# Cross-attention and a mixture of experts on one core: softmax row sums from ScalarE's exponentials, their logarithm added to the maximum, and three chunks' maxima beside the projections

## The chip, the cores and the metric

The kernel runs on one core of a Trainium2 chip. The metric is the device time of one execution in microseconds. A core has TensorE (PE, matrix multiplications into PSUM), VectorE (DVE), ScalarE (ACT), GpSimd (POOL) and SyncE (SP, which here issues DMAs); each runs its own list of instructions in order, and they wait for each other by semaphores.

## The reference

The input x has 8 sequences of 512 tokens and 512 features, and so has the context. All is float32.

```
xn = layernorm(x)
Q = xn @ Wq.T + bq;  K = ctx @ Wk.T + bk;  V = ctx @ Wv.T + bv     # 16 heads of 32
attn = softmax(Q K^T / sqrt(32));  x = x + (attn V) @ Wo.T + bo
xn = layernorm(x)
scores = softmax(xn @ router.T + rb);  top 2 of 8 experts per token
x = x + sum over the two: score * (down( (up + 1) * gate * sigmoid(1.702 gate) ) + bias)
```

## The kernel before

The program has three stages one after the other: attention (`attention_stage`), the routing, and the experts. The change is in the first alone. It goes over the 8 sequences ("batches", b). Within one, the 512 features are four chunks c of 128 (four heads h of 32 each), and the 512 tokens four tiles t or k of 128.

**Precision.** Where float32 would be slow, a value is split in a high part of type float32r and a low part, and a product is made of three passes (`PASSES`, hi by hi, hi by lo, lo by hi). Each of q and k is split after its projection (`qk_hi` on ScalarE, line 430, and `qk_lo` on VectorE, line 595), and DMAs stack the parts in `qs[c]` and `ks[c]`, three by 32 rows of the contraction, so that one matmul of 96 rows is a head's product (`stack_hi` on SP's queue, `stack_lo` on GpSimd's, line 765). Two more rows of the contraction, 98 in all, hold the high and low part of minus the row maximum in `qs` and ones in `ks`: so the subtraction of the maximum is done by the matmul.

**Scores are made twice.** First by query: `row_max` (line 276) makes the scores of one head and 128 queries against 512 keys; VectorE takes their negated maximum (`reduce_max`, line 609) into `negmax`. Chunks 0 and 1 do it in pairs of query tiles, 128x1024 in a two-bank PSUM tile `st`; chunks 2 and 3 row by row, 128x512 in `work`. When a chunk's 16 maxima are there, `turn_max` transposes them, `m_hi_copy` and `m_lo_sub` split them, and `send_max` writes them into the two rows of `qs`. Then by key: `exp_scores` (line 291) makes the transposed scores of 128 keys, and ScalarE their exponential (line 448, with the scale 1/sqrt(32)) into `pt`. `weigh_values` multiplies these by v (`o_ps`, line 304) and by ones (`sum_ps`, line 309), the latter giving the row sums in the same layout. At a chunk's end `copy_sums` (line 457) copies both to SBUF, and in four pieces VectorE takes the reciprocal and multiplies (`divide`, lines 619 and 622), and the result is split into `oT` (`o_hi`, line 464; `o_lo`, line 627). `project_out` (line 326) multiplies by Wo: chunks 0 to 2 of all four token tiles first, then chunk 3.

**Order.** The order is written out by hand. `STEPS` lists twelve projections, k0 v0 q0 q1 k1 v1 q2 k2 v2 q3 k3 v3. Each is issued in four quarters, and after each quarter the function calls `next(fill)`: a generator that puts one item of other work there. The same generator skeleton stands on TensorE, ScalarE and VectorE, so that their orders agree. During the projections it puts in the previous batch's router work (transposes of `xln`, the logits, their sum), then chunk 0's maxima beside q2, k2, v2 and chunk 1's beside q3, k3, v3. During the weighing the items follow the 16 tiles (c, k), four places to a tile: the maxima of chunks 2 and 3, and the pieces of the division. In the last chunk's tiles VectorE also makes the next batch's statistics and LayerNorm (`norm_stats`, `ln1`, line 566), after which come the pieces that are left.

**Rings.** PSUM has 8 banks: `work` 2, `st` 2 tiles of two banks, `o_ps` and `sum_ps` one each. The uses of `work` and of `st` are listed in order (`use_work`, `use_st`), each takes the other buffer of two in turn, and a matmul waits until the use before the last has been read.

Of the kernel before, what the change touches and what calls it, by code (L numbers as in the profile page):

```python
# [14 lines left out]
P = 128  # L15
# [34 lines left out]
def attention_stage(nc, x, ctx_t, w_t, bq, bk, bv, bo, router_wt, router_b, out, xln_dram, logits, ident):  # L50
# [7 lines left out]
    with ExitStack() as ctx:  # L58
# [31 lines left out]
        o_sum = sb("o_sum", [P, 2, S])  # L90
        parts = sb("parts", [P, S])
        ones = sb("ones", [P, HD])
# [12 lines left out]
        o_ps = psum("o_ps", [P, S])  # L105
        sum_ps = psum("sum_ps", [P, S])

        STEPS = [(n, c) for c in range(C) for n in ("kvq" if c == 0 else "qkv")]
# [3 lines left out]

        bs = range(B)
        s_w, s_init, s_first_x, s_raw_w, s_split, s_split_lo = (sem(n) for n in (
            "w_in", "consts_made", "first_x_in", "raw_w_in", "w_hi_made", "w_lo_made"))
# [12 lines left out]
        MAXES = [(b, c, h, t) for b in bs for c in range(C) for h, t in (PAIRS if c < 2 else ROWS)]  # L128
# [13 lines left out]
        copied = Mark(sem("copied"), [(b, c, i) for b in bs for c in range(C) for i in (1, 0)])  # L142
        oT_hi_made = Mark(sem("oT_hi_made"), [(b, c, t) for b in bs for c in range(C) for t in range(T)])
# [12 lines left out]
        inverted = Mark(sem("inverted"), [(b, c, t) for b in bs for c in range(C) for t in range(T)])  # L156
        divided = Mark(sem("divided"), [(b, c, t) for b in bs for c in range(C) for t in range(T)])
        oT_lo_made = Mark(sem("oT_lo_made"), [(b, c, t) for b in bs for c in range(C) for t in range(T)])
# [15 lines left out]
        def use_st_for_router(b):  # L174
            for half in range(2):
                use_st((b, "xln", half), xlnT_made, (b, half))
            use_st((b, "logits"), parts_made, b)
            use_st((b, "sum"), logits_out, b)

        for b in bs:  # L180
            for n, c in STEPS:
                use_work((b, n, c), *((v_made, (b, c)) if n == "v" else (qk_lo_made, (b, n, c))))
                if (n, c) == ("q", 3):
                    use_work((b, "turn", 0), m_lo_made, (b, 0))
            for c in range(1, C):
                use_work((b, "turn", c), m_lo_made, (b, c))
                if c < C - 1:
                    for h, t in ROWS:
                        use_work((b, "max", c + 1, h, t), maxed, (b, c + 1, h, t))
# [4 lines left out]
            if b:  # L194
                use_st_for_router(b - 1)
            for c in range(2):
                for h, t in PAIRS:
                    use_st((b, "max", c, h, t), maxed, (b, c, h, t))
# [5 lines left out]
        use_st_for_router(B - 1)  # L204
# [3 lines left out]
        def on_pe(e):  # L208
# [15 lines left out]
            def turn_xln(b, half):  # L224
                i = take(st_ring, (b, "xln", half))
# [43 lines left out]
            def row_max(b, c, h, t):  # L269
                ring, n = (st_ring, 2) if c < 2 else (work_ring, 1)  # L270
# [8 lines left out]
            def turn_max(b, c):  # L279
                i = take(work_ring, (b, "turn", c))  # L280
                e.wait_ge(maxed.sem, maxed[(b, c, *(PAIRS if c < 2 else ROWS)[-1])])
                e.transpose(work[i][0:GROUP * T, 0:P], negmax[:, c, :], ident[:, :]).then_inc(max_turned.sem, 1)
# [13 lines left out]
            def weigh_values(b, c, k, fill):  # L296
                if k == 0:
                    e.wait_ge(v_made.sem, v_made[b, c])
                    if (b, c) != (0, 0):
                        e.wait_ge(copied.sem, copied[b if c else b - 1, c - 1 if c else C - 1, 0])  # L300
                e.wait_ge(exped.sem, exped[b, c, k, 1])
                for h in range(GROUP):
                    rows = slice(HD * h, HD * (h + 1))
                    e.matmul(o_ps[rows, :], v[:, k, c * P + HD * h:c * P + HD * (h + 1)], pt[k % 2][:, h, :],  # L304
                             start=(k == 0), stop=(k == T - 1))
                next(fill, None)
                for h in range(GROUP):
                    rows = slice(HD * h, HD * (h + 1))
                    ins = e.matmul(sum_ps[rows, :], ones[:, :], pt[k % 2][:, h, :], start=(k == 0), stop=(k == T - 1))  # L309
# [3 lines left out]
            def project_out(b):  # L313
# [4 lines left out]
                for chunks in (range(C - 1), range(C - 1, C)):  # L318
                    for t in range(T):
                        for c in chunks:  # L320
                            if c == C - 1:
                                e.wait_ge(oT_lo_made.sem, oT_lo_made[b, c, t])
                            elif t == 0:
                                e.wait_ge(oT_lo_made.sem, oT_lo_made[b, c, T - 1])
# [7 lines left out]
            def beside_first(b):  # L332
                for _ in range(7):
                    yield
                for half in range(2):
                    if b:
                        turn_xln(b - 1, half)
                    yield
                    yield
                yield  # L340
                if b:
                    route_logits(b - 1)
                for _ in range(4):
                    yield
                if b:
                    sum_logits(b - 1)
                yield

            def beside_second(b):
                yield  # L350
                for h, t in PAIRS:
                    row_max(b, 0, h, t)
                    yield

            def beside_third(b):
# [1279 lines left out]
```

## Time and profile before

| | us |
|---|---|
| median of 3 runs | 1897.19 (1895.81 to 1897.5) |
| profiled execution: its time | 1896.04 |
| profiled execution: its span | 1894.3 |
| TensorE, VectorE, ScalarE, GpSimd busy | 1735.4, 1366.4, 667.7, 469.7 |
| exponentials (line 448), 256 | 249.4 |
| row maxima of 128x512 (line 609), 256 | 175.0 |
| row maxima of 128x1024 (line 609), 128 | 151.6 |
| reciprocals (line 619), 128 | 120.9 |
| matmuls into sum_ps (line 309) | 135.0 |

Matmuls are pipelined: the duration of one in the trace is longer than the distance from its start to the next one's start, and the distances are what adds up. The same holds for instructions of ScalarE and VectorE that follow each other without a wait.

### The profile page before, as it was taken

What the parts mean: (1) busy time and instruction counts of PE and PEld (TensorE: products, weight loads), DVE (VectorE), ACT (ScalarE), POOL (GpSimd) and SP (SyncE); (2) the same over time, 40 slices, a digit from 0 to 9 for tenths busy, and PEclk for the clock granted to TensorE, in tenths of its full rate; (3) what the DMA queues carried; (4) which work ended last, traced back from release to release, by engine and by line L of the source; (5) the groups of instructions that cost most, each with busy time, mean ns of one, the idle gap of its engine ahead of it and who ended that gap; (6) DMA issues with size and microseconds to landing.
All of it is one profiled execution on the core that took longest, in us unless ns stands there. A gap on an engine that the chain in (4) does not pass through costs nothing. (4 is left out here: it accounts for less than half of the span.)

```text
span 1894.3 us, 31367 instructions
## 1 busy us (share of the span) xinstructions
PE 1735.4 (92%) x10597; PEld 1253.6 (66%) x10597; DVE 1366.4 (72%) x2488; ACT 667.7 (35%) x1107; POOL 469.7 (25%) x628
## 2 busy tenths in 40 slices
PE   5989989989989999899899827999999999999996
PEld 4537547447356365375474427998989889889895
DVE  3775775775766757757757587778787888888874
ACT  2252342441532622523524404233434343434221
POOL 3212113013022032121122002343333333334332
PEclk9999999999999999999999958999999999999998
DMA  6404306206117025044052042253636535636322
GB/s 220 127 2 135 111 1 169 77 25 171 52 44 202 2 76 170 2 119 127 1 141 62 36 145 80 69 218 101 227 92 224 201 124 191 216 123 230 92 79 78
DMA packets 103797, 216.06 MB, mean 114 GB/s; under 512 B 25936, under 2 KB 26960, under 8 KB 103632
## 3 DMA queue, kind: packets, MB, share of 16 engines
q1 hardware_dynamic: 75696, 135.27, 22.4%
q0 software_dynamic: 27936, 78.73, 13.2%
q8 instruction: 86, 1.41, 0.3%
q14 instruction: 79, 0.65, 0.1%
HBM read 204.19 MB, written 37.36 MB: 128 GB/s over the span
## 5 line engine op out<-in xcount | busy, mean ns | idle before, releaser
L1265 PE MATMUL gu_ps<-xgT_hi,wg_hi 128*128 128x256 f32 x1248 | 354.9, 284 | 0.0
L1265 PE MATMUL gu_ps<-xgT_hi,wg_lo 128*128 128x256 f32 x1248 | 351.7, 282 | 0.0
L1265 PE MATMUL gu_ps<-xgT_lo,wg_hi 128*128 128x256 f32 x1248 | 351.5, 282 | 0.0
L448 ACT ACTIVATE pt<-st 128x1024 f32<-128x1024 f32 x256 | 249.4, 1018 | 152.2 <-PE st L291 152.2
L1265 PEld LDWEIGHTS gu_ps<-xgT_hi,wg_hi 128*128 128x128 f32 x1248 | 235.5, 189 | 0.0
L1265 PEld LDWEIGHTS gu_ps<-xgT_lo,wg_hi 128*128 128x128 f32 x1248 | 235.5, 189 | 0.0
L1265 PEld LDWEIGHTS gu_ps<-xgT_hi,wg_lo 128*128 128x128 f32 x1248 | 235.3, 189 | 0.0
L609 DVE TENSOR_REDUCE negmax<-work 128x1 f32<-128x512 f32 x256 | 175.0, 689 | 62.4 <-PE work L276 61.3
L1325 ACT ACTIVATE sig<-gate 128x256 f32<-128x256 f32 x156 | 65.0, 417 | 303.1 <-DVE gate L1377 303.1
L291 PE MATMUL st<-qs,ks 98*128 98x512 f32 x512 | 165.1, 416 | 5.8 <-ACT pt L448 5.1
L609 DVE TENSOR_REDUCE negmax<-st 128x2 f32<-128x1024 f32 x128 | 151.6, 1218 | 25.6 <-PE st L276 23.9
L1503 POOL DMA_INDIRECT out<-acc,idx x78 | 77.3, 991 | 346.8 <-DVE acc L1413 346.8
L1278 PE MATMUL d_ps<-wd_hi,hid_hi 128*128 128x512 f32 x312 | 127.3, 408 | 22.9 <-DVE acc L1410 22.9
L755 POOL TENSOR_TENSOR var_eps<-mv,eps_col 128x4 f32<-128x4 f32 x16 | 3.2, 197 | 571.5 <-DVE mv L563 571.4
L260 PE MATMUL work<-ctxT,wk 128*128 128x512 f32 x256 | 128.4, 610 | 13.0 <-DVE q_lo L595 8.7
L304 PE MATMUL o_ps<-pt,v 128*32 128x512 f32 x1024 | 136.2, 604 | 2.3 <-issue 2.3
L619 DVE RECIPROCAL o_sum<-o_sum 128x128 f32<-128x128 f32 x128 | 120.9, 944 | 23.9 <-ACT o_sum L457 23.9
L291 PEld LDWEIGHTS st<-qs,ks 98*128 98x128 f32 x512 | 88.7, 189 | 70.7 <-ACT pt L448 38.3
L309 PE MATMUL sum_ps<-pt,ones 128*32 128x512 f32 x1024 | 135.0, 598 | 0.0
L257 PEld LDWEIGHTS work<-wv,ctxT 128*128 128x128 f32 x1024 | 123.1, 192 | 11.2 <-issue 7.7
L1278 PE MATMUL d_ps<-wd_lo,hid_hi 128*128 128x512 f32 x312 | 125.3, 401 | 0.0
L1278 PE MATMUL d_ps<-wd_hi,hid_lo 128*128 128x512 f32 x312 | 125.1, 401 | 0.0
(195 smaller groups left out, 3170.5 us busy)
## 6 DMA issues: line engine op xcount, KB each, us to landing
raw_g<-w_gate_up SPq DMA_DIRECT2D x39, 2048.0 KB
raw_d<-w_down SPq DMA_DIRECT2D x39, 1024.0 KB
ks<-k_hi SPq DMA_DIRECT2D x256, 64.0 KB, 2.1
qs<-q_hi SPq DMA_DIRECT2D x256, 64.0 KB, 2.5
bd<-b_down SPq DMA_DIRECT2D x39, 256.0 KB
x_in<-x SPq DMA_DIRECT2D x8, 1024.0 KB, 5.3
ctxT<-ctx_t SPq DMA_DIRECT2D x8, 1024.0 KB, 5.7
ks<-k_lo POOLq DMA_DIRECT2D x128, 64.0 KB, 2.4
```

The costliest lines, as they stand in the source:

```text
L257: ins = e.matmul(work[i][:, k * P:(k + 1) * P], ctxT[:, kk, k * P:(k + 1) * P], wv[:, kk, c * P:(c + 1) * P], start=(kk == 0), stop=(kk == ...
L260: ins = e.matmul(work[i][:, :], wk[:, k, c * P:(c + 1) * P], ctxT[:, k, :], start=(k == 0), stop=(k == C - 1))
L291: ins = e.matmul(st[i][:, j, :], ks[c][0:3 * HD + 2, h, k * P:(k + 1) * P], qs[c][0:3 * HD + 2, h, :], start=True, stop=True)
L304: e.matmul(o_ps[rows, :], v[:, k, c * P + HD * h:c * P + HD * (h + 1)], pt[k % 2][:, h, :], start=(k == 0), stop=(k == T - 1))
L309: ins = e.matmul(sum_ps[rows, :], ones[:, :], pt[k % 2][:, h, :], start=(k == 0), stop=(k == T - 1))
L448: e.activation(pt[k % 2][:, 2 * p:2 * p + 2, :], st[st_ring.bank[b, "exp", c, k, p]][:, :, :], ACT.Exp, scale=scale).then_inc(exped.sem, 1)
L609: e.tensor_reduce(negmax[:, c, h * T + t:h * T + t + n], src, AX.X, ALU.max, negate=True).then_inc(maxed.sem, 1)
L619: e.reciprocal(o_sum[:, 1, cols], o_sum[:, 1, cols]).then_inc(inverted.sem, 1)
L1265: ins = e.matmul(gu_ps[n % GU_BANKS][:, part, :], wg[s][pw][:, k, cols], xgT[s][px][:, k, :], start=(k == 0 and m == 0), stop=(k == KD - 1 ...
L1278: ins = e.matmul(d_ps[j][:, :], hid[s][px][:, k, j * P:(j + 1) * P], wd[s][pw][:, k, :], start=(k == 0 and m == 0), stop=(k == KF - 1 and ...
L1325: e.activation(sig[f % 2][:, :], gate[f % 2][:, :], ACT.Sigmoid, scale=ALPHA).then_inc(sig_made.sem, 1)
L1503: e.indirect_dma_start(out=out_rows, out_offset=slot_rows(i, j), in_=acc[i % 2][:, j, :], in_offset=None).then_inc(scattered.sem, 16)
```

## The change

- `sum_ps`, its matmuls, `ones`, `o_sum`, the copies, the reciprocals and the multiplications are removed. The 256 matmul groups of `weigh_values` into `o_ps` stay, and `o_ps` has two buffers now, by the parity of the chunk. One copy (`o_hi`) and one subtraction (`o_lo`) of 128x512 make `oT` straight from `o_ps`.
- The row sums are made on the scores by query: after VectorE's maximum, ScalarE takes the exponential of the same PSUM tile in place, with the negated maximum as its bias, and its accumulator output gives the sum of a row (`row_sums`: 64 per batch, 128x512 each). The PSUM buffer is free only after that.
- Per chunk, ScalarE takes the logarithm of the 16 columns of sums (`ln_of_sums`) and VectorE subtracts it from the negated maximum (`add_ln`); this `shift` is what is transposed and sent. So the exponentials by key are normalised already.
- The scale 1/sqrt(32) goes into Wq and bq at the start.
- Three chunks' row maxima (24 pairs) stand beside the projections instead of two; chunk 3's alone stand row by row in the weighing. The order of steps is k0 q0 q1 k1 k2 q2 q3 k3 v0 v1 v2 v3. A quarter counts from 0 to 47; chunk c's pairs stand at 12(c + 1) + 0, 1, 3, 4, 6, 7, 9, 10, the turns of chunks 0 and 1 at 26 and 38, the router's work at 8, 10, 14 and 17.
- GpSimd sends the maxima of chunks 0 and 1 after all its stacking; SP stores the previous batch's rows after k1.

```diff
-        STEPS = [(n, c) for c in range(C) for n in ("kvq" if c == 0 else "qkv")]
+        STEPS = [(n, c) for c in range(C) for n in ("kq" if c % 2 == 0 else "qk")] + [("v", c) for c in range(C)]
+        PAIR_AT = {12 * (c + 1) + n // 2 * 3 + n % 2: (c, *PAIRS[n]) for c in range(C - 1) for n in range(len(PAIRS))}
+        TURN_AT = {12 * (c + 2) + 2: c for c in range(C - 2)}
+        ROUTER_AT = {8: ("xln", 0), 10: ("xln", 1), 14: "logits", 17: "sum"}
...
             def weigh_values(b, c, k, fill):
                 if k == 0:
-                    e.wait_ge(v_made.sem, v_made[b, c])
-                    if (b, c) != (0, 0):
-                        e.wait_ge(copied.sem, copied[b if c else b - 1, c - 1 if c else C - 1, 0])
+                    e.wait_ge(v_made.sem, v_made[b, C - 1])
+                    if c >= 2:
+                        e.wait_ge(oT_lo_made.sem, oT_lo_made[b, c - 2])
+                    elif b:
+                        e.wait_ge(oT_lo_made.sem, oT_lo_made[b - 1, c + 2])
                 e.wait_ge(exped.sem, exped[b, c, k, 1])
-                for h in range(GROUP):
-                    rows = slice(HD * h, HD * (h + 1))
-                    e.matmul(o_ps[rows, :], v[:, k, c * P + HD * h:c * P + HD * (h + 1)], pt[k % 2][:, h, :],
-                             start=(k == 0), stop=(k == T - 1))
                 next(fill, None)
                 for h in range(GROUP):
                     rows = slice(HD * h, HD * (h + 1))
-                    ins = e.matmul(sum_ps[rows, :], ones[:, :], pt[k % 2][:, h, :], start=(k == 0), stop=(k == T - 1))
+                    ins = e.matmul(o_ps[c % 2][rows, :], v[:, k, c * P + HD * h:c * P + HD * (h + 1)], pt[k % 2][:, h, :],
+                                   start=(k == 0), stop=(k == T - 1))
...
+            def row_sums(b, c, h, t):
+                ring, n = (st_ring, 2) if c < C - 1 else (work_ring, 1)
+                i = ring.bank[b, "max", c, h, t]
+                e.wait_ge(maxed.sem, maxed[b, c, h, t])
+                for j in range(n):
+                    at = h * T + t + j
+                    scores = st[i][:, j, :] if n == 2 else work[i][:, :]
+                    e.activation(scores, scores, ACT.Exp, bias=negmax[:, c, at:at + 1],
+                                 accum_out=sums[:, c, at:at + 1]).then_inc(summed.sem, 1)
+
+            def ln_of_sums(b, c):
+                e.wait_ge(summed.sem, summed[(b, c, *ROWS[-1])])
+                e.activation(ln_sums[:, c, :], sums[:, c, :], ACT.Ln).then_inc(ln_made.sem, 1)
...
+            def beside_projections(b):        # ScalarE
+                for quarter in range(C * len(STEPS)):
+                    if b and quarter in ROUTER_AT:
+                        what = ROUTER_AT[quarter]
+                        if what == "logits":
+                            parts_copy(b - 1)
+                        elif what != "sum":
+                            xln_copy(b - 1, what[1])
+                    if quarter - 1 in PAIR_AT:
+                        row_sums(b, *PAIR_AT[quarter - 1])
+                    if quarter + 1 in TURN_AT:
+                        ln_of_sums(b, TURN_AT[quarter + 1])
+                    if quarter in TURN_AT:
+                        m_hi_copy(b, TURN_AT[quarter])
                     yield
...
+            def beside_weighing(b):           # ScalarE
+                yield
+                ln_of_sums(b, C - 2)
+                yield
+                m_hi_copy(b, C - 2)
+                yield
+                for h, t in ROWS:
                     yield
+                    row_sums(b, C - 1, h, t)
                     yield
+                ln_of_sums(b, C - 1)
                 yield
+                m_hi_copy(b, C - 1)
                 yield
...
+            def add_ln(b, c):
+                e.wait_ge(ln_made.sem, ln_made[b, c])
+                e.tensor_tensor(shift[:, c, :], negmax[:, c, :], ln_sums[:, c, :], ALU.subtract).then_inc(shift_made.sem, 1)
...
+            def o_lo(b, c):
+                e.wait_ge(oT_hi_made.sem, oT_hi_made[b, c])
+                e.tensor_tensor(oT[1][:, c, :], o_ps[c % 2][:, :], oT[0][:, c, :].bitcast(F32), ALU.subtract).then_inc(oT_lo_made.sem, 1)
...
-                    if (n, c) == ("q", 3):
-                        send_max(e, b, 0)
-                send_max(e, b, 1)
+                for c in range(C - 2):
+                    send_max(e, b, c)
```

## Rows read from the trace of the kernel before

**Rows 1.** The page's totals: busy us (share of the span), count.
```profile
PE 1735.4 (92%) x10597; PEld 1253.6 (66%) x10597; DVE 1366.4 (72%) x2488; ACT 667.7 (35%) x1107; POOL 469.7 (25%) x628
```
**Rows 2.** Busy time by stretch: stretch, length, engines, TensorE clock, DMA.
```profile
400.01:419.92 19.91, 15.79 (x68) 12.41 (x65) 15.44 (x24) 2.99 (x7) 3.78 (x1) 0.83 0.00 1
419.92:472.65 52.73, 51.50 (x276) 37.91 (x274) 32.65 (x42) 9.69 (x14) 17.97 (x36) 1.00 0.61 173
472.65:533.21 60.56, 59.14 (x358) 22.70 (x356) 42.63 (x80) 36.89 (x53) 2.94 (x5) 1.00 0.13 43
405.00:411.00 6.00, 5.30 (x13) 4.19 (x14) 4.32 (x9) 1.70 (x4) 0.00 (x0) 0.52 0.01 3
```
**Rows 3.** Timeline of TensorE, output projection: start, us, line, count, idle before.
```profile
401.27 0.40 PE L326 MATMUL work<-wo_hi,xT_hi 128*128 128x512 f32 x1
405.70 0.80 PE L326 MATMUL work<-wo_hi,oT_hi 128*128 128x512 f32 x1 [4.03 <-DVE xT_hi L627]
...
418.12 1.97 PE L221 MATMUL st<-ident,x_in 128*128 128x128 f32 x16
419.92 3.60 PE L260 MATMUL work<-ctxT,wk 128*128 128x512 f32 x8
...
1065.78 0.51 PE L326 MATMUL work<-wo_hi,oT_hi 128*128 128x512 f32 x1
...
1076.80 0.40 PE L326 MATMUL st<-wo_hi,xT_hi 128*128 128x512 f32 x1
```
**Rows 4.** Timeline of VectorE around the same output projection.
```profile
395.14 2.47 DVE L558 BATCH_NORM_STATS2 stats<-x_in 128x6 f32<-128x512 f32 x4
...
399.31 6.14 DVE L566 TENSOR_SCALAR x_in<-x_in,mv,rstd 128x512 f32<-128x512 f32 x4 [1.43 <-POOL rstd L757]
405.37 0.28 DVE L627 TENSOR_TENSOR xT_hi<-o_sum,oT_hi 128x128 fp32r<-128x128 f32 x1
...
421.34 2.33 DVE L582 TENSOR_TENSOR xT_lo<-st,xT_hi 128x1024 fp32r<-128x1024 f32 x2
```
**Rows 5.** Timeline of TensorE, a tile of the weighing without row maxima.
```profile
515.30 1.20 PE L291 MATMUL st<-qs,ks 98*128 98x512 f32 x4
516.43 1.06 PE L304 MATMUL o_ps<-pt,v 128*32 128x512 f32 x8
517.32 1.04 PE L309 MATMUL sum_ps<-pt,ones 128*32 128x512 f32 x8
518.29 0.50 PE L291 MATMUL st<-qs,ks 98*128 98x512 f32 x1
```
**Rows 6.** Groups of ScalarE by shape, 387 to 517: busy us, mean ns, idle.
```profile
L448 ACT ACTIVATE pt<-st 128x1024 f32<-128x1024 f32 x31 | 30.2, 1018 | 19.0 <-PE st L291 19.0
...
L430 ACT ACTIVATE q_hi<-work,bq_col 128x512 fp32r<-128x512 f32 x4 | 2.7, 687 | 11.0 <-PE work L263 11.0
...
L457 ACT ACTIVATE o_sum<-sum_ps 128x512 f32<-128x512 f32 x4 | 2.4, 598 | 10.4 <-DVE xT_hi L627 7.9 <-PE sum_ps L309 2.5
...
L438 ACT ACTIVATE m_hi<-work 16x128 fp32r<-16x128 f32 x4 | 1.0, 254 | 4.9 <-PE work L282 4.9
```
**Rows 7.** Timeline of ScalarE, two exponentials in sequence.
```profile
387.05 1.92 ACT L448 ACTIVATE pt<-st 128x1024 f32<-128x1024 f32 x2
```
**Rows 8.** Groups of ScalarE over the whole span: both table loads.
```profile
L513 ACT ACT_TABLE_LOAD x1 | 1.3, 1283 | 2.0 <-PEq L1578 2.0
L1325 ACT ACT_TABLE_LOAD x1 | 1.3, 1283 | 0.0
```
**Rows 9.** Timeline of TensorE, projections: quarters of k, pairs of row maxima.
```profile
447.56 1.02 PE L260 MATMUL work<-ctxT,wk 128*128 128x512 f32 x2
448.02 1.02 PE L276 MATMUL st<-ks,qs 96*128 96x512 f32 x2
448.89 1.02 PE L260 MATMUL work<-ctxT,wk 128*128 128x512 f32 x2
...
459.68 0.62 PE L276 MATMUL st<-ks,qs 96*128 96x512 f32 x2
460.14 0.40 PE L263 MATMUL work<-xT_hi,wq_hi 128*128 128x512 f32 x1
```
**Rows 10.** Timeline of VectorE, the maximum of the pair of 459.68.
```profile
460.34 1.22 DVE L609 TENSOR_REDUCE negmax<-st 128x2 f32<-128x1024 f32 x1 [1.28 <-PE st L276]
```
**Rows 11.** Timeline of GpSimd, issuing the stack of a low part of q.
```profile
433.44 1.96 POOL L765 DMA_DIRECT2D qs<-q_lo  x4 [4.95 <-DVE q_lo L595]
```
**Rows 12.** DMA issues, 387 to 517: count, KB each, median us to landing.
```profile
qs<-q_lo POOLq DMA_DIRECT2D x16, 64.0 KB, 2.3
```

More of the change, by code:

```diff
@@ L172, in use_st, with use_st_for_router @@
             st_uses.append((key, len(st_uses) % 2, mark, event))
[L174 to L178, printed above, removed]
+        ROUTER_AT = {8: ("xln", 0), 10: ("xln", 1), 14: "logits", 17: "sum"}
+        def use_st_for_router(b, what):
+            over = {"logits": (parts_made, b), "sum": (logits_out, b)}
+            use_st((b, what), *over.get(what, (xlnT_made, (b, what[1]))))
         for b in bs:
-            for n, c in STEPS:
+            for i, (n, c) in enumerate(STEPS):
                 use_work((b, n, c), *((v_made, (b, c)) if n == "v" else (qk_lo_made, (b, n, c))))
-                if (n, c) == ("q", 3):
[L184 to L189, printed above, removed]
+                for quarter in range(C * i, C * (i + 1)):
+                    if quarter in TURN_AT:
+                        use_work((b, "turn", TURN_AT[quarter]), m_lo_made, (b, TURN_AT[quarter]))
+            use_work((b, "turn", C - 2), m_lo_made, (b, C - 2))
+            for h, t in ROWS:
+                use_work((b, "max", C - 1, h, t), summed, (b, C - 1, h, t))
+            use_work((b, "turn", C - 1), m_lo_made, (b, C - 1))
             for t in range(2):
@@ L203, in attention_stage @@
                 use_st((b, "out", t), x2_made, (b, t))
-        use_st_for_router(B - 1)
+        for what in ROUTER_AT.values():
+            use_st_for_router(B - 1, what)
         work_ring, st_ring = Ring(work_uses), Ring(st_uses)
@@ L224, in turn_xln @@
             def turn_xln(b, half):
-                i = take(st_ring, (b, "xln", half))
+                i = take(st_ring, (b, ("xln", half)))
                 for j in range(2):
@@ L416, in xln_copy @@
                 e.wait_ge(xln_turned.sem, xln_turned[b, half])
-                e.activation(pt[0][:, 2 * half:2 * half + 2, :], st[st_ring.bank[b, "xln", half]][:, :, :],
+                e.activation(pt[0][:, 2 * half:2 * half + 2, :], st[st_ring.bank[b, ("xln", half)]][:, :, :],
                              ACT.Identity).then_inc(xlnT_made.sem, 1)
@@ L473, in beside_first, with beside_projections @@
-            def beside_first(b):
-                for _ in range(7):
+                e.activation(oT[0][:, c, :], o_ps[c % 2][:, :], ACT.Identity).then_inc(oT_hi_made.sem, 1)
+            def beside_projections(b):
+                for quarter in range(C * len(STEPS)):
+                    if b and quarter in ROUTER_AT:
+                        what = ROUTER_AT[quarter]
+                        if what == "logits":
+                            parts_copy(b - 1)
[5 more added lines that the diff above has]
+                        ln_of_sums(b, TURN_AT[quarter + 1])
+                    if quarter in TURN_AT:
+                        m_hi_copy(b, TURN_AT[quarter])
+                    yield
@@ L511, in on_act @@
             e.wait_ge(s_raw_w, 32)
-            for w, raw in ((wq, pt[0]), (wo, pt[1])):
-                e.activation(w[0][:, :, :], raw[:, :, :], ACT.Identity).then_inc(s_split, 1)
+            for w, raw, factor in ((wq, pt[0], scale), (wo, pt[1], 1.0)):
+                e.activation(w[0][:, :, :], raw[:, :, :], ACT.Identity, scale=factor).then_inc(s_split, 1)
             for b in bs:
@@ L604, in reduce_max @@
             def reduce_max(b, c, h, t):
-                n, ring, banks = (2, st_ring, st) if c < 2 else (1, work_ring, work)
+                n, ring, banks = (2, st_ring, st) if c < C - 1 else (1, work_ring, work)
                 i = ring.bank[b, "max", c, h, t]
```

277 lines of the change are left out of this document (80 added, 197 removed).

## The prediction, made before the change was run

> **What bounds the kernel now.** I read the page's totals first, then the busy time by stage, then the order of work on each engine in one batch. TensorE is the busiest engine, at 92% of the span, with VectorE at 72% and ScalarE at 35% [rows 1]. One batch of the attention stage takes 133.2 us, from 400.01 to 533.21, in three stages [rows 2]: the output projection with the transposes of the next x, 19.9 us; the projections of k, v and q, 52.7; the weighing, 60.6. In the last two TensorE is busy 98% of the time, so there its work sets the time. The first is different: the output projection stands still for 4.03 us, waiting for the low part of oT [rows 3], because VectorE first runs the statistics and the LayerNorm of the next x, from 395.14 to 405.37 [rows 4]. Around this stall the granted clock is 0.52 on average [rows 2], the lower of the two levels (1.2 and 2.4 GHz) for a part of it. In the last batch, which has no next x, the same 48 matmuls run from 1065.78 to 1076.80, 11.3 us with the last one's slot [rows 3]. ScalarE is busy 9.7 of 52.7 us in the projections and 36.9 of 60.6 in the weighing [rows 2].
>
> **What is removed, stage by stage.** I count from the time of the profiled execution, 1896.04 us (its span is 1894.3; the median of the runs shown is 1897.19, so 1.2 us above it).
>
> Output projection: the four reciprocals, multiplications and splits of the last chunk become one copy and one subtraction. VectorE reaches the next x's statistics right after the low part of chunk 2, about four tiles before the end of the weighing. Statistics, the wait for rstd (1.43) and the LayerNorm take 10.2 us [rows 4]; four tiles take some 9 (4 x 2.1, and the last weighing). The low part of chunk 3 is then ready about 4 us after the last tile, and 36 matmuls of chunks 0 to 2 at 0.235 us (11.3 over 48) cover 8.5 us. So the stall and the low clock behind it go. 11.3 + 1.8 for the transposes (from 418.12 to the end of the stage at 419.92) [rows 2, 3] + 0.4 of gaps + 0.3 waiting for the low half of the next x = 13.8 us instead of 19.9: 6.1 gained, in 7 batches, since the last had no stall. That is 42.7 us.
>
> Weighing: today a tile without row maxima takes 2.99 us (515.30 to 518.29), of which the sum matmuls are 0.97 (517.32 to 518.29) [rows 5]. Without them, and with 16 row maxima instead of 32, TensorE needs 2.0 us in such a tile, and some 2.5 where two row maxima of 0.23 stand in it (a pair takes 0.46, from 459.68 to 460.14) [rows 9]. ScalarE now sets the pace. An exponential of 128x1024 takes 1.02 us by itself and 0.92 in sequence (two end after 1.92; 1.92 - 1.00) [rows 6, 7]. A row's sum is a new operation: an exponential of 128x512 with a bias column and an accumulator output. No row shows the output. Call its slot R. The nearest row is q_hi, 128x512 with a bias column, 0.687 us, which is 0.59 with the same overlap of 0.1 [rows 6]. That is the lower bound: the accumulator costs nothing. The upper one adds the whole of the shortest ScalarE row, m_hi with 128 columns (0.254), and no overlap: 0.94. I take the accumulator as m_hi without its columns: 0.254 - 128 x 0.00082 = 0.15 (0.00082 us a column: 1018 less 598 ns over 512 columns is 0.82 ns) [rows 6], so R = 0.74, which of the two ends lies nearer to the q_hi row. Then: start 2.0 (the last pair of chunk 2 goes out 1.4 us before the projections end, and its bank is held 3.5); first tile 1.84; eight tiles with rows, 8 x (1.84 + 2 x 0.74) = 26.6; seven without at 2.1 (TensorE's 2.0 and a handoff), 14.7; three copies of o_ps on ScalarE, 0.5 each and one of them partly beside TensorE, 1.2; two logarithms and two m_hi at 0.16 after overlap, 0.7; the last weighing, 0.9 and a handoff, 1.0. Sum 48.0 instead of 60.6: 12.6 gained per batch. With R = 0.59 it is 45.6, with 0.94 it is 51.2. VectorE, busy 42.6 of 60.6 us there today [rows 2], loses the divisions and half of the row maxima and isn't late.
>
> **What is added: the projections.** Here are now 24 pairs of rows instead of 16, and each pair's bank is held for more. Before: matmuls to the start of the reduction 0.66 us (459.68 to 460.34; the matmuls end at 460.30, so a handoff costs 0.04), reduction 1.22 [rows 9, 10], then free. Now two exponentials follow: hold = 0.66 + 1.22 + two handoffs, 0.08, + 2R + the last one's overlap, 0.1 = 3.54 us. Two banks make two pairs per 3.54 us. TensorE's own time for two pairs and the three quarters between them: a quarter of k with its pair takes 1.33 (447.56 to 448.89) of which the pair is 0.46 [rows 9], so with k 3 x 0.87 + 0.94 = 3.55, with v about the same, with q (three matmuls of 0.235) 3.04. So in k and v the ring just keeps up, and every disturbance of it is paid. I wrote the order of the three engines out, quarter by quarter. TensorE's bare work is 52.7 + 8 pairs x 0.5 - 1.1 of today's wait for q_lo = about 55. The stalls that I find on top:
> - quarter 12: the pairs of chunk 0 start one step after q0. Its low part is ready 1.6 us after the projection, GpSimd's four issues take 1.96 and the landing 2.3 [rows 11, 12], against q1, the xln transposes and a k quarter (5.3): 0.9;
> - the router's two uses of the same ring (the xln transposes before them have it to themselves), at quarters 14 and 17, wait for sums ahead of them, and ScalarE's copy of the logits stands before the sums of pair 13: 0.8 + 1.3 + 1.3;
> - the q quarters of q2, with the splits of q and k in between: 1.2;
> - quarter 26: the transposition of the maxima now waits for reduction, sums, logarithm and addition of the last pair of chunk 0, queued behind pair 24: 1.4. Behind it k3 waits for q3's split, which stands behind these sums on ScalarE and behind the addition on VectorE: 1.6;
> - chunk 1's last two pairs 0.7, its turn at quarter 38 1.0, v2's bank 0.4, chunk 2's last pair 0.4.
>
> That is 11 at R = 0.69, where I wrote it out, and 12 at R = 0.74 (12 rounds of the ring by 0.1). Projections: 67.0 instead of 52.7, 14.3 lost per batch. With R = 0.59, 63.9; with R = 0.94, 12 x 0.4 more, 71.9.
>
> Costed at nothing: the order k, q, q, k with v last (the low half of x is made at 423.67, and k0 covers from 419.92 until 423.52, so q0 waits the 0.3 counted above [rows 3, 4]; v is needed only at the first weighing); the later send of the maxima of chunk 0 on GpSimd (some 3 us for two sends, done about 5 us before ScalarE's next m_hi; if it were late, ScalarE's queue, with the sums behind it, would wait); the store of xln one step earlier on SP's queue, behind which the stacking of k2 and q2 lies, needed more than 10 us later; the scale put into wq at the start, the same two instructions as before; k's and q's stacks for chunk 1, three steps old.
>
> **Sum.** 8 x (12.6 - 14.3) = -13.6, and 42.7: a gain of 29 us, 1867 us. At R = 0.59: 8 x (15.0 - 11.2) + 42.7 = 73, 1823. At R = 0.94: 8 x (9.4 - 19.2) + 42.7 = -36, 1932.
>
> **Rivals.**
> 1. The hold is lighter (R near 0.59, or ScalarE's and VectorE's turns fall better than I wrote them): 1823. For it: handoffs of 0.04 leave nothing between the engines to lose. If the ring never bound at all, the projections would take 56 us, and the time would be 1896 - 42.7 - 8 x (12.6 - 3.3) = 1779. Against that: 3.54 us of hold against 3.04 in q.
> 2. The sums are dear, R above 0.83: there the gain is spent (0.1 of R is worth 8 x (2.4 + 1.6) = 32 us). Place: the bank held in the projections and ScalarE's queue in the weighing. Up to 1932. For it: the unknown accumulator. Against: 0.83 is already 0.24 above the activation's slot.
> 3. The logarithm and the exponential don't share a table. Then each of the 32 logarithms brings a load and one back, 64 x 1.28 us [rows 8] = 82 us on the queue that holds the ring: 1867 + 82 = 1949. It decides from 0.9 us per logarithm. Against: in the attention stage's trace Identity and Exp run after a single load [rows 8].
>
> The Trainium skill bears on this last one ("ScalarE: Activation LUTs", Table sets: the hidden batching unit): one set, natural_log_exp_and_others, holds both, so exponential after logarithm needs one load; and "ScalarE activation tables: per-element evaluation and per-set limits" (Table sets in the compiler and the runtime) says that the back end takes the set with the longest run. By that rule rival 3 doesn't happen. The first page gives 2.66 us for a switch with its drain; by that price the rival would stand at 1867 + 170. No row before has a logarithm, so that the rule holds here is not shown.
>
> **How the numbers follow.** Forecast, 1840 to 1893: 0.55. Rival 1: 0.15 for 1800 to 1840, 0.04 for less. No measurable change, within 0.2% (3.8 us, about what a measurement of this kernel can tell from none): 0.04. Rival 2: 0.13. Rival 3: 0.09. Faster 0.74, same 0.04, slower 0.22. The range goes from 1815 to 1925: it leaves out rival 3, the last of rival 2, and the lightest of rival 1. The forecast's own range is 1840 to 1893. With the 1.2 us between execution and median I give 1868.
>
> **What would show it.** Right: no wait of 4 us in the output projection, its clock 1.0, and 14 us for that stage; 48 us for the weighing with ScalarE the busiest engine; about 67 us for the projections, with TensorE waiting for ScalarE's sums before the pairs, at the two turns and before k3; sums of about 0.7 us plus a short accumulator entry. Wrong: a table load beside the logarithms; R off by more than 0.1; the stall in the output projection still there, because VectorE comes to the next x later than I think; projections under 60 us.

## The result, and the profile after

The changed kernel takes 2046.92 us (median of 4 runs, 2044.52 to 2048.85), the one before 1897.35 on the same chip: a ratio of 1.0788 [1.0769, 1.0807], 7.9% slower. I had forecast 1868. The profiled execution has a span of 2047.1 us, and a mean granted clock of 0.911 where the kernel before had 0.962.

The page's totals (busy us, share, instructions) after; [rows 1] are those of before:

```profile
PE 1725.3 (84%) x9573; PEld 1249.2 (61%) x9573; DVE 1205.9 (59%) x2105; ACT 1064.6 (52%) x2067; POOL 471.4 (23%) x627
```

TensorE's share fell from 92 to 84%, ScalarE's rose from 35 to 52%. No engine is at its limit over the whole; something waits. The same batch as in [rows 2], by its three stages (stretch, length, busy time of TensorE, its weight loads, VectorE, ScalarE, GpSimd, then granted clock, DMA share, GB/s):

```profile
459.89:473.20 13.31, 13.23 (x68) 10.76 (x65) 8.20 (x12) 1.27 (x2) 2.02 (x1) 1.00 0.01 2
473.20:552.66 79.46, 63.60 (x292) 43.66 (x290) 42.91 (x53) 47.76 (x113) 18.98 (x38) 0.89 0.42 120
552.66:610.09 57.43, 46.77 (x210) 16.90 (x210) 19.53 (x34) 49.99 (x79) 3.76 (x3) 0.88 0.12 38
```

| stage, us | before | forecast | after |
|---|---|---|---|
| output projection and transposes | 19.9 | 13.8 | 13.3 |
| projections | 52.7 | 67.0 | 79.5 |
| weighing | 60.6 | 48.0 | 57.4 |
| one batch | 133.2 | 128.8 | 150.2 |

The first stage is as forecast. The other two are longer by 12.5 and 9.4 us, and 8 x 21.4 is 171 of the 179 us that were missing. Both have a clock well below 1.0, which in [rows 2] only the first stage had.

These groups of ScalarE are new; nothing in [rows 6, 8] is like them (line, operation, count, busy us, mean ns, idle time before and its releaser):

```profile
L438 ACT ACTIVATE st<-st,negmax 128x512 f32<-128x512 f32 x384 | 252.7, 658 | 157.7 <-DVE negmax L571 156.8
...
L443 ACT ACT_TABLE_LOAD x32 | 41.1, 1283 | 0.6
...
L438 ACT ACTIVATION_READ_ACCUMULATOR st<-st,negmax 128x1 f32 x384 | 76.2, 198 | 0.0
...
L438 ACT ACT_TABLE_LOAD x16 | 20.5, 1283 | 0.3
L427 ACT ACT_TABLE_LOAD x16 | 20.5, 1283 | 13.8 <-PE o_ps L313 13.7
```

There are 64 table loads in attention: one ahead of each of the 32 logarithms (line 443), and one ahead of the exponential that follows each, half of those being row sums (438) and half exponentials of the weighing (427). This is rival 3. ScalarE in order of time shows both new things, the sum's slot and the round trip of a logarithm (start, us, instruction, idle time before it):

```profile
400.94 0.66 ACT L438 ACTIVATE st<-st,negmax 128x512 f32<-128x512 f32 x1 [0.44 <-DVE negmax L571]
401.53 0.19 ACT L438 ACTIVATION_READ_ACCUMULATOR st<-st,negmax 128x1 f32 x1
401.62 0.65 ACT L438 ACTIVATE st<-st,negmax 128x512 f32<-128x512 f32 x1
...
405.90 1.28 ACT L443 ACT_TABLE_LOAD   x1
407.19 0.22 ACT L443 ACTIVATE ln_sums<-sums 128x16 f32<-128x16 f32 x1
407.43 1.28 ACT L427 ACT_TABLE_LOAD   x1
```

From one sum to the next, 400.94 to 401.62, are 0.68 us: R, with the accumulator's entry partly under the next exponential. The logarithm of 0.22 us holds ScalarE for 2.8.

What TensorE waited for in this batch (total us, times, longest):

```profile
PE work L288 <- DVE shift L576: 12.2, 4, 5.3
PE st L282 <- DMA qs<-q_hi: 4.3, 1, 4.3
PE st L282 <- ACT st L438: 2.6, 5, 1.0
PE work L266 <- DVE q_lo L557: 2.5, 1, 2.5
PE st L297 <- ACT st L438: 1.2, 2, 0.9
...
PE st L251 <- ACT st L438: 1.1, 1, 1.1
```

The rings that I had costed at length cost 3.7 us in the projections: 2.6 before pairs (line 282) and 1.1 before the router's logits (line 251). In the weighing they cost another 2.3: 1.2 before the first exponentials (line 297) and 1.1 before a row of chunk 3. The largest wait is for `shift`, the maxima with the logarithm added, at the four transpositions: 2.46, 2.38, 2.03 and 5.30 us in their order. The next is for chunk 0's `q_hi` to land. TensorE in order of time shows these stalls and, at the end, tiles of the weighing:

```profile
489.77 1.19 PE L282 MATMUL st<-ks,qs 96*128 96x512 f32 x2 [4.26 <-DMA qs<-q_hi]
...
520.94 2.07 PE L266 MATMUL work<-ctxT,wk 128*128 128x512 f32 x2 [2.54 <-DVE q_lo L557]
...
565.17 1.31 PE L297 MATMUL st<-qs,ks 98*128 98x512 f32 x4
...
568.33 1.31 PE L297 MATMUL st<-qs,ks 98*128 98x512 f32 x4
...
591.82 0.37 PE L288 MATMUL work<-ident,shift 128*16 128x128 f32 x1 [5.30 <-DVE shift L576]
...
597.46 1.20 PE L297 MATMUL st<-qs,ks 98*128 98x512 f32 x4
...
599.59 1.37 PE L297 MATMUL st<-qs,ks 98*128 98x512 f32 x4
```

A tile with two row sums takes 3.16 us (565.17 to 568.33), one without 2.13 (597.46 to 599.59). In the row at 520.94 the two matmuls take 2.07 us, where two of the same shape took 1.02 before [rows 9]. The stretches right behind three of the stalls, in the columns of the stages:

```profile
489.70:495.70 6.00, 5.93 (x16) 2.65 (x16) 2.45 (x2) 1.45 (x4) 0.00 (x0) 0.59 0.32 82
520.90:526.70 5.80, 5.76 (x11) 2.96 (x12) 2.53 (x3) 2.90 (x8) 1.97 (x4) 0.62 0.51 136
591.80:597.40 5.60, 5.58 (x21) 1.65 (x21) 0.28 (x1) 3.48 (x4) 0.00 (x0) 0.54 0.01 3
```

TensorE is busy all through them at a granted clock of 0.54 to 0.62, that is for most of each at 1.2 GHz instead of 2.4. So these stalls seem to be paid twice, by their length and by the low clock behind them; e2 and e11 below test this.

What holds q_hi up is to be seen in SyncE's queue of DMA issues, after:

```profile
477.56 4.97 SPq L742 DMA_DIRECT2D ks<-k_hi  x8
482.62 10.18 SPq L742 DMA_DIRECT2D qs<-q_hi  x16
```

Eight issues take 4.97 us, 0.62 each. The queue does k0's eight until 482.5, then q0's, the first half of the sixteen in the second row, to about 487.6, and these land at 489.7. The same price stood in the same queue of the kernel before, a row that I had not drawn on:

```profile
424.27 4.96 SPq L815 DMA_DIRECT2D ks<-k_hi  x8
```

### The profile page after: what moved, and what is told of

Its sections match the earlier page's. It is cut to its first block and busy times, and to the rows that moved or that the text cites. A ratio compares the mean times of both kernels' runs of the same rounds, so it can differ in the third digit from the quotient of the medians.

```text
span 2047.1 us, 29620 instructions
## 1 busy us (share of the span) xinstructions
PE 1725.3 (84%) x9573; PEld 1249.2 (61%) x9573; DVE 1205.9 (59%) x2105; ACT 1064.6 (52%) x2067; POOL 471.4 (23%) x627
## 5 line engine op out<-in xcount | busy, mean ns | idle before, releaser
L438 ACT ACTIVATE st<-st,negmax 128x512 f32<-128x512 f32 x384 | 252.7, 658 | 157.7 <-DVE negmax L571 156.8
L571 DVE TENSOR_REDUCE negmax<-st 128x2 f32<-128x1024 f32 x192 | 234.0, 1222 | 136.4 <-PE st L282 135.1
L282 PE MATMUL st<-ks,qs 96*128 96x512 f32 x384 | 177.9, 548 | 57.6 <-DMA qs<-q_hi 38.0
L297 PE MATMUL st<-qs,ks 98*128 98x512 f32 x512 | 181.1, 461 | 10.8 <-ACT st L438 9.3
L266 PE MATMUL work<-ctxT,wk 128*128 128x512 f32 x256 | 159.3, 733 | 21.7 <-DVE q_lo L557 17.1
L313 PE MATMUL o_ps<-pt,v 128*32 128x512 f32 x1024 | 156.4, 687 | 4.6 <-ACT pt L427 4.6
L282 PEld LDWEIGHTS st<-ks,qs 96*128 96x128 f32 x384 | 73.4, 217 | 124.3 <-issue 78.7
L263 PEld LDWEIGHTS work<-wv,ctxT 128*128 128x128 f32 x1024 | 134.5, 200 | 12.3 <-DVE v L563 5.3
L571 DVE TENSOR_REDUCE negmax<-work 128x1 f32<-128x512 f32 x128 | 87.4, 688 | 90.3 <-PE work L282 90.3
L263 PE MATMUL work<-wv,ctxT 128*128 128x128 f32 x1024 | 137.6, 285 | 0.3 <-DVE v L563 0.3
```

Of the source, the lines that this page charges most:

```text
L263: ins = e.matmul(work[i][:, k * P:(k + 1) * P], ctxT[:, kk, k * P:(k + 1) * P], wv[:, kk, c * P:(c + 1) * P], start=(kk == 0), stop=(kk == ...
L266: ins = e.matmul(work[i][:, :], wk[:, k, c * P:(c + 1) * P], ctxT[:, k, :], start=(k == 0), stop=(k == C - 1))
L282: ins = e.matmul(to, qs[c][0:3 * HD, h, (t + j) * P:(t + j + 1) * P], ks[c][0:3 * HD, h, :], start=True, stop=True)
L297: ins = e.matmul(st[i][:, j, :], ks[c][0:3 * HD + 2, h, k * P:(k + 1) * P], qs[c][0:3 * HD + 2, h, :], start=True, stop=True)
L313: ins = e.matmul(o_ps[c % 2][rows, :], v[:, k, c * P + HD * h:c * P + HD * (h + 1)], pt[k % 2][:, h, :], start=(k == 0), stop=(k == T - 1))
L438: e.activation(scores, scores, ACT.Exp, bias=negmax[:, c, at:at + 1], accum_out=sums[:, c, at:at + 1]).then_inc(summed.sem, 1)
```

## The experiments

My theory after the traces: three things cost the time, the loads (64 x 1.28 = 82 us by themselves), the new waits (`shift`, and q_hi on SP's queue) and the clock that falls behind them. The rival: the sums themselves, in rings and ScalarE's queue, cost it, and the waits are only where it shows.

**One table.** ScalarE's table is loaded by hand once at the start, with the set that holds both functions:

```
+            e.add_instruction(mybir.InstLoadActFuncSet(..., engine=Activation, act_func_set_id=6))
             e.wait_ge(s_raw_w, 32)
```

> The changed kernel with one table that holds both Exp and Ln loaded at the start, so that the 64 loads beside the logarithms go. Theory A (the loads are the largest part of the loss: 64 x 1.28 us stand on the way, and after each the clock of TensorE is low for some us): 1935 to 1965 us, no load in the attention stage, the waits at the turns 1.3 us shorter each. Rival B (the ring is what holds, the loads lie beside waits that stay): above 2010 us.

1960.33 us, 1.0334 [1.0317, 1.0352] of before: 87 us less than the change. No load stands beside the logarithms any more:

```profile
375.00 1.95 ACT L427 ACTIVATE pt<-st 128x1024 f32<-128x1024 f32 x2
376.85 0.21 ACT L443 ACTIVATE ln_sums<-sums 128x16 f32<-128x16 f32 x1
376.95 1.02 ACT L427 ACTIVATE pt<-st 128x1024 f32<-128x1024 f32 x1
```

The round trip went from 2.8 us to 0.1. The loads, with what they drag behind them, explain half of the missing 179. The rest stands in this kernel's projections, weighing, and waits:

```profile
441.10:513.43 72.33, 60.47 (x292) 41.63 (x290) 42.80 (x53) 42.08 (x109) 18.91 (x38) 0.95 0.46 132
513.43:567.71 54.28, 46.48 (x210) 16.40 (x210) 19.62 (x34) 44.58 (x75) 3.75 (x3) 0.91 0.11 40
...
549.30:555.10 5.80, 5.80 (x22) 1.57 (x21) 0.28 (x1) 2.21 (x3) 0.00 (x0) 0.50 0.01 3
```

```profile
PE work L288 <- DVE shift L577: 6.5, 4, 3.9
...
PE st L282 <- DMA qs<-q_hi: 4.2, 1, 4.2
...
PE work L266 <- DVE q_lo L558: 1.1, 1, 1.1
```

The wait for shift halved, its longest still 3.9 us, and the stretch behind that one runs at 0.50. The wait for q_hi is untouched.

**The clock by itself.** Throwaway matmuls fill the stalls at the turns and before the first pair, and the waits stay (the one before k3 is left unfilled). This is done first on the changed kernel (e2), then, with fewer, on the one-table kernel (e11):

```
                 i = take(work_ring, (b, "turn", c))
+                for _ in range(9 if c < 2 else (8 if c == 2 else 22)):   # second: 4, 4, 2, 16
+                    e.matmul(work[i][:, :], wq[0][:, 0, 0:P], wq[0][:, 1, :], start=True, stop=True)
                 e.wait_ge(shift_made.sem, shift_made[b, c])
...
+                if (c, h, t) == (0, 0, 0):
+                    for _ in range(18):
+                        e.matmul(st[i][:, 0, :], wq[0][:, 0, 0:P], wq[0][:, 1, :], start=True, stop=True)
                 e.wait_ge(stacked[c].sem, stacked[c][b])
```

> The changed kernel with throwaway matmuls of 128x512 (0.235 us each) on TensorE before its five long waits of a batch: 18 before the first pair of chunk 0, 9 before the turns of chunks 0 and 1, 8 and 22 before those of chunks 2 and 3. The waits stay as long as they are, TensorE only works through them. Theory A (after a wait of 2 us or more the clock falls for some 6 us, which costs up to 2 us of TensorE's own time each, in the projections where it is near the limit): 1990 to 2015 us and a granted clock near 1.0 in the attention stage. Rival C (the clock's fall is hidden, since ScalarE and the ring set the pace): 2040 to 2055 us with the clock high all the same.

2000.52 us, 1.0554 [1.0532, 1.0575]: 46 less than the change, the mean clock up from 0.911 to 0.966.

> e1_one_table with throwaway matmuls before its long waits (18 before chunk 0's first pair, 4, 4, 2 and 16 before the four turns). Theory A on the clock: the low clock after the two waits of about 4 us costs some 1 to 2 us each, so 15 to 35 us less than 1960; granted clock of the attention stage near 1.0. Rival C (hidden): within 8 us of 1960.

1916.82 us, 1.0107 [1.009, 1.0124]: 43.5 less than one table alone, clock 0.97 instead of 0.94, and more than the 15 to 35 that I expected. Work that yields nothing made the kernel 2.2% faster. The weighing went from 54.3 us to:

```profile
495.19:545.22 50.03, 46.64 (x229) 18.68 (x229) 19.54 (x34) 44.50 (x75) 3.76 (x3) 1.00 0.13 44
```

Filler can't shorten a wait by itself; what changed is the clock, here 1.00 instead of 0.91.

**The sums themselves.** One table, and chunks 0 to 2 leave out the exponentials of their row sums (one-column exponentials signal in their place):

```
+                if n == 2:
+                    for j in range(n):
+                        at = h * T + t + j
+                        e.activation(sums[:, c, at:at + 1], negmax[:, c, at:at + 1], ACT.Exp, scale=0.0)...
+                    return
```

> As e1_one_table, and the row sums of chunks 0 to 2 are left out (one column of ones is written instead of the two exponentials), so that a pair's PSUM buffer is free about 0.3 us after its maximum. It leaves out part of the softmax. Theory A: the hold of the ring costs 8 to 12 us of a batch's projections; 65 to 95 us less than e1_one_table. Rival D (the ring hardly binds, the turns and the DMAs do): less than 30 us below e1_one_table.

1904.24 us, 1.0038 [1.0024, 1.0052]: 56 below one table, less than expected. The projections go to 66.7 us a batch. So 384 of the 512 sums cost 56 us, some of which the forecast had counted, and even without them the projections are 14 us longer than before. As the loads cost 87 us and were no part of this, the rival is not the main cause of the miss; it is no small one either.

**Cover for q_hi by another order of steps.** v0 is put between q0 and the pairs:

```
-        STEPS = [(n, c) for c in range(C) for n in ("kq" if c % 2 == 0 else "qk")] + [("v", c) for c in range(C)]
+        STEPS = [(n, int(c)) for n, c in "k0 q0 v0 q1 k1 k2 q2 v1 q3 k3 v2 v3".split()]
```

> The changed kernel with the steps k0 q0 v0 q1 k1 k2 q2 v1 q3 k3 v2 v3 (GpSimd sends chunk 0's maxima after q3's stack), so that 3.6 us more lie between q0 and chunk 0's first pair. Theory E (the 4.3 us wait before that pair is SP's issuing: 16 descriptors of k0 and q0 at 0.62 us one after the other): the wait is below 1 us, and the time 2000 to 2020 us. Rival (the transfers themselves are late, for lack of bandwidth): the wait stays above 3 us and the time within 1% of 2047.

2046.89 us, 1.0790 [1.0764, 1.0816]: nothing, and a miss. v0 only took the place of q1 between q0 and the first pair, so it added hardly any cover. In the batch looked at the wait is 3.0 us instead of 4.3, put down to the issue itself:

```profile
PE st L282 <- issue: 3.0, 1, 3.0
```

The run says nothing for or against the queue; the edit was badly made.

**The issues on two queues.** One table, and GpSimd issues the second copy of chunk 0's high parts, which SP did before:

```
-                for part in places:
+                for part in places[:1] if c == 0 else places:          # SP
...
+                if c == 0:                                              # GpSimd, ahead of the low part
+                    e.wait_ge(qk_hi_made.sem, qk_hi_made[b, n, c])
+                    for r in range(GROUP):
+                        e.dma_start(dst[HD * part:HD * (part + 1), r, :]..., hi[n][c % 2][...]...).then_inc(stacked_too.sem, 16)
```

> As e1_one_table, and for chunk 0 alone the second copy of the high parts is issued by GpSimd, so that SP issues 4 descriptors of k0 and of q0 instead of 8, and GpSimd 8 of 0.5 us. Theory E (the wait before chunk 0's first pair is issuing time in a queue): q0's last part now lands by GpSimd's queue, some 1.4 us sooner; the wait falls from 4.4 to about 3 us, and the time by 8 to 20 us, to 1940 to 1952. Rival F (the landing is late for another reason, the transfers' bandwidth or q0's split): the wait and the time stay within 4 us of e1_one_table, 1960.

1937.48 us, 1.0213 [1.0196, 1.023]: 23 less than one table. The wait went from 4.2 to 1.9 us, and is now for GpSimd's low part:

```profile
PE st L285 <- DMA qs<-q_lo: 1.9, 1, 1.9
```

So the wait was the queue's issuing, 0.62 us a descriptor. 2.3 us x 8 are 18 of the 23; that the rest is the clock is argued and was not tried here.

**The turns later.** One table; each transposition of the maxima stands later, by one quarter in the projections and by four and five places (a tile or a little more) in the weighing, its result goes into the `o_ps` bank that is idle then, and the logarithm goes ahead of the next chunk's sums:

```
-        TURN_AT = {12 * (c + 2) + 2: c for c in range(C - 2)}
+        TURN_AT = {12 * (c + 2) + 3: c for c in range(C - 2)}
...
-                e.transpose(work[i][0:GROUP * T, 0:P], shift...
+                e.transpose(o_ps[TURN_IN[c]][0:GROUP * T, 0:P], shift...
...
+                    if quarter + 3 in TURN_AT:                  # ScalarE, ahead of row_sums
+                        ln_of_sums(b, TURN_AT[quarter + 3])
...
+                    if at == 7:                                 # TensorE, places in the weighing (before: 3 and 37)
+                        turn_max(b, C - 2)
+                    if at == 42:
+                        turn_max(b, C - 1)
```

> As e1_one_table, and the transposition of a chunk's shifts comes later on TensorE, where logarithm and addition are done (quarters 27 and 39; places 7 and 42 of the weighing instead of 3 and 37), the logarithm stands ahead of the next chunk's sums, and the result goes into an idle o_ps bank instead of the ring of work. Theory G (the turns' waits, 6.2 us of a batch, k3's wait of 1.1 and the low clock behind them are the second part of the loss): 8 to 11 us of a batch, 1870 to 1900 us, no wait for shift over 0.3 us. Rival H (ScalarE sets the pace and the waits only move to other places): above 1935 us.

1926.88 us, 1.0163 [1.0146, 1.018]: 33.5 less than one table, not the 60 to 90 expected. The wait for shift is gone, but others grew in its place:

```profile
PE st L278 <- DMA qs<-q_hi: 4.1, 1, 4.1
PE st L278 <- ACT st L435: 4.1, 6, 1.5
...
PE st L296 <- ACT pt L424: 1.9, 3, 1.4
```

The ring's wait for ScalarE went from 2.6 in the changed kernel to 4.1: TensorE, no longer held at the turns, now meets the sums. That is one part of the shortfall. The other is the clock, as two weighings of this one execution show:

```profile
224.78:273.74 48.96, 42.47 (x210) 15.35 (x211) 19.48 (x34) 44.23 (x75) 3.75 (x3) 1.00 0.14 44
357.15:411.47 54.32, 47.92 (x211) 17.51 (x211) 19.59 (x34) 44.69 (x75) 3.76 (x3) 0.87 0.12 40
```

TensorE's waits in the two are the same, down to the tenth, and none is longer than 1.4 us; in the 14 us ahead of each the order and the clock, 1.00, are the same too. Yet the second takes 5.4 us more, at a clock of 0.87. Two of the eight weighings went as the first, six took 52.9 to 54.4 us at 0.87. So the low clock costs time by itself, and in this kernel it also comes without a wait of 2 us or more. What decides between the two was not tried.

> Both edits, of e5 and of e6. If they add up: 8 to 20 us below e6_turns_late.

Both edits together: 1904.25 us, 1.0042 [1.0025, 1.0059], 56.1 less than one table, where the two alone give 22.9 + 33.5 = 56.4. So the two gains add up.

**The pairs later and further apart.** The turns late, one table, SP issuing all again; the 24 pairs are spread over quarters 16 to 46, with one more step ahead of them:

```
+        STEPS = [(s[0], int(s[1])) for s in "k0 q0 q1 v0 k1 k2 q2 q3 k3 v1 v2 v3".split()]
+        PAIR_AT = {16 + (8 * c + n) * 4 // 3: (c, *PAIRS[n]) for c in range(C - 1) for n in range(len(PAIRS))}
+        TURN_AT = {30: 0, 41: 1}
+        ROUTER_AT = {8: ("xln", 0), 10: ("xln", 1), 12: "logits", 15: "sum"}
```

> As e6_turns_late with the steps k0 q0 q1 v0 k1 k2 q2 q3 k3 v1 v2 v3 and the 24 pairs spread evenly, three to four quarters, from quarter 16 on; the router's logits and sum at 12 and 15, ahead of the pairs. Theory E: four quarters, 3.6 us of work, stand in place of the wait for chunk 0's stacks, and the ring has no router use in it: 25 to 50 us below e6_turns_late, no wait for a DMA over 1 us. Rival: the ring, with fewer quarters between its pairs, takes back what the wait gives: within 10 us of e6_turns_late.

1866.86 us, 0.9853 [0.9832, 0.9875]: 60 less than the turns alone, more than expected, and faster than the kernel before.

> e8_pairs_later without its one table: the 64 loads are back. Theory A (each load holds ScalarE where ScalarE or its ring sets the pace, wherever the turns stand): 80 to 90 us more than e8_pairs_later, 1947 to 1957 us. Rival (with the turns late, a logarithm and its loads lie beside other work): less than 40 us more.

The same without the single table: 1971.54 us, 1.0386 [1.0369, 1.0404]. The loads cost 105 us here against 87 in the changed kernel, in both more than their own 82 us. With them the mean clock falls from 0.965 to 0.933; how the 105 divide between the loads, the waits behind them and the clock was not tried.

> e8_pairs_later with the last turn one place earlier (41 instead of 42): the wait for the DMA of chunk 3's maxima, 1.2 us of a batch, goes, and a shorter one for the shift may come. 2 to 10 us less than 1867; if the shift is later than I think, no change.

The last turn at place 41 instead of 42, in TensorE's, ScalarE's and VectorE's order (`-  if at == 42:` `+  if at == 41:`): 1856.67 us, 0.978 [0.9764, 0.9796], the fastest, 2.2% below the kernel before. Its stages and TensorE's waits in one batch:

```profile
395.25:408.55 13.30, 13.20 (x68) 10.77 (x65) 8.20 (x12) 1.27 (x2) 2.01 (x1) 1.00 0.01 2
408.55:472.31 63.76, 57.83 (x293) 40.88 (x291) 42.40 (x53) 42.20 (x109) 18.91 (x38) 1.00 0.52 149
472.31:521.56 49.25, 42.55 (x213) 15.45 (x211) 20.04 (x34) 44.06 (x75) 3.76 (x3) 1.00 0.14 44
```

```profile
PE st L278 <- ACT st L435: 5.7, 10, 1.5
PE st L296 <- ACT pt L424: 2.2, 4, 1.4
...
PE st L296 <- DMA qs<-m_lo: 0.9, 1, 0.9
```

No wait is longer than 1.5 us, and the clock is 1.00 in all three stages. The gain over e8 is mostly the clock again: there four of the eight weighings took 51.0 to 52.4 us, at 0.93 to 0.97, and four 49.5 at 1.00, with waits that differ by 0.1 us between one of each; here seven took 49.2 and the first 53.8, at 0.87. 63.8 and 49.3 us stand beside the 67.0 and 48.0 of my forecast. The balance that I had argued (12.6 gained in the weighing, 14.3 lost in the projections) is there, at 11.3 and 11.1, once the loads, the waits at the turns and the early first pair are out of the way. But this is another schedule than the one I priced, so that its nearness to my numbers doesn't confirm the single terms.

## Why the prediction was wrong, step by step

- **Output projection, 13.8: right.** 13.3 us, clock 1.00, no wait. VectorE in order of time shows the statistics ahead of the stage's start at 459.89, and the low part of chunk 3 ready at 464.18, under the 36 matmuls of chunks 0 to 2; the forecast had said some 4 us after the last tile [rows 4]:

```profile
453.23 2.47 DVE L520 BATCH_NORM_STATS2 stats<-x_in 128x6 f32<-128x512 f32 x4
...
457.40 6.17 DVE L528 TENSOR_SCALAR x_in<-x_in,mv,rstd 128x512 f32<-128x512 f32 x4 [1.43 <-POOL rstd L685]
463.50 0.68 DVE L585 TENSOR_TENSOR xT_hi<-o_ps,oT_hi 128x512 fp32r<-128x512 f32 x1
```

- **R = 0.74: right within its bounds,** 0.68. The nearest row, q_hi with 0.69 [rows 6], was almost the slot itself. With 0.68 a tile with rows is 1.84 + 1.36 = 3.20 by my formula, measured 3.16; one without was 2.1, measured 2.13. The rings bind, as said, for 3.7 us in the projections, where my terms for them (quarters 14 and 17, q2, the last pairs of chunks 1 and 2) add up to 5.7. Rival 2 didn't happen.
- **"Two logarithms and two m_hi at 0.16": failed; rival 3 happened.** 64 loads, as that rival counted them, worth 87 us by the run with one table. It was given 0.09. The evidence against it was that Identity and Exp run after one load [rows 8], which says nothing of a pair with a logarithm. The Trainium skill's rules that I set beside it ("ScalarE: Activation LUTs", Table sets: the hidden batching unit; "ScalarE activation tables: per-element evaluation and per-set limits", Table sets in the compiler and the runtime) are half borne out: a set with both functions exists, since with one table a single load serves the whole attention stage, but this program's build did not choose it and switched around every logarithm. How it chooses is not shown here. The Trainium skill's 2.66 us a switch ("ScalarE: Activation LUTs", What ACT_TABLE_LOAD costs) is not borne out either: a load takes 1.283 us and the next instruction starts at its end (407.19 after 405.90), and even by the experiments, with all that waits behind, it is 1.35 and 1.64 each (87 and 105 us over 64).
- **"Quarter 12: 0.9": the term was mis-sized, 4.26.** I priced GpSimd's four issues and the landing, and left out SP's sixteen, 10 us of one queue that k0 and q0 share. A row with that price, 4.96 us for eight, was in the trace of before. Worth 23 us for the half that was taken out, and e8, which starts the pairs later, has no such wait at all.
- **The turns: right in the projections but for the loads, failed in the weighing.** "Quarter 26: 1.4" and quarter 38's 1.0 came out as 2.46 and 2.38 us; with one table the two together are 2.0. k3's wait for q3's split, "1.6", came out as 2.54, and as 1.1 with one table. For the two turns in the weighing I counted ScalarE's time alone and no wait of TensorE. But TensorE carries out its order: it stands at the transposition until sum, logarithm and addition are done, 2.03 and 5.30 us, and with one table still 4.5 together, 3.9 of them at the last one. All four together are 12.2 us a batch with loads, 6.5 without.
- **The clock: not in the sum at all.** I took the fall to half clock as a part of the stall that goes [rows 2], and didn't ask what the new stalls of 2 to 5 us would do to it. Filling them gave 43.5 us on the one-table kernel, 46 on the changed one. These are not a further part beside the two waits, since a change that takes a wait can take its clock with it. It needn't: with the turns late the waits for shift were gone, and six of eight weighings still ran at 0.87.
- **The sum.** 179 us were missing. From the changed kernel down: 87 the loads, 33.5 the turns, 60 the pairs' places, 10 the last turn; 190 in all, which ends 11 below the forecast. By the stages of the two traces the 60 are 44 in the projections, where the wait for q_hi of 4.1 us a batch went (8 x 4.1 = 33), and 15 in the weighing, whose order that edit leaves alone and where four instead of six ran at less than the full clock. Of the last turn's 10, some 7 are in the weighings, by their clock.
- **Rival 1** didn't happen either. The projections of e10, 63.8 us, lie at my value for the light hold (63.9), but that is chance: R is 0.68 there too, and the pairs stand elsewhere. By my own 12 rounds of the ring that value would have been 63.4, not 63.9.

## What to carry to other kernels

When a change brings a function to ScalarE that the kernel never used, count the loads in the compiled instruction stream before anything else, and load by hand a set that holds all. An instruction of TensorE at the end of a chain over other engines (sum, logarithm, addition, then transposition) needs other work between it and the last of these, or their latency is TensorE's wait; here a tile or a little more was enough, and one place fewer was better still. Look at TensorE's granted clock stage by stage, and in several batches, beside the waits: a low clock has a price of its own, and equal batches can differ by it. A step that is moved closer to the transfers that it needs must be priced against each queue that issues them, descriptor by descriptor.

## What the runs showed of the hardware

- An accumulator output comes as an entry of its own, ACTIVATION_READ_ACCUMULATOR, of 0.198 us on `st` and 0.235 on `work`; about half lies under the next activation, so that a sum's slot is 0.68 us.
- A table load takes 1.283 us with no visible drain around it.
- In the stretches behind stalls of 2.5 to 5.3 us the granted clock was 0.50 to 0.62, with TensorE busy all through. Throwaway matmuls in the stalls bought back 2.2%.
- The clock also fell where no wait was longer than 1.4 us: of the weighings of one execution with the same waits, two took 49.0 us at 1.00 and six 52.9 to 54.4 us at 0.87. In the fastest kernel one weighing of the eight ran at 0.87 and seven at 1.00.
- An issue of a DMA costs 0.62 us on SP's queue (8 in 4.97) and 0.49 on GpSimd's (four in 1.96) [rows 11].
